# Attention with row maxima on one core: two PSUM banks for row scores and three for column scores, instead of three and two

## What is computed

```python
cov = jnp.einsum('bhsd,bhtd->bhst', qc, kc) / D
var_comp = q_var[..., :, None] * k_var[..., None, :] / D
attn = jax.nn.softmax(cov + var_comp, axis=-1)      # (32, 16, 256, 256)
out = jnp.einsum('bhst,bhtd->bhsd', attn, v)
```

## Time and profile before

| | |
|---|---|
| median of 3 runs | 1299.82 us (1298.62 to 1304.07) |
| profiled execution | 1300.59 us, of which the span from the first to the last instruction 1298.3 us |
| PE busy | 1127.0 us, 87% of the span |
| DVE busy | 989.6 us, 76% |
| ACT busy | 796.9 us, 61% |
| POOL busy | 375.9 us, 29% |
| mean granted TensorE clock | 0.972 of full speed |

### The profile page before, as it was taken

How to read it: one execution, slowest core, us unless ns; L and a number is a source line. 1 busy time by engine, 2 the same in 40 slices (tenths; PEclk the granted TensorE clock), 3 DMA queues, 4 the chain that set the end, 5 groups by cost and what they waited for, 6 DMA issues and landing times.

```text
span 1298.3 us, 33300 instructions
## 1 busy us (share of the span) xinstructions
PE 1127.0 (87%) x11462; PEld 669.0 (52%) x11462; DVE 989.6 (76%) x2827; ACT 796.9 (61%) x1440; POOL 375.9 (29%) x644
## 2 busy tenths in 40 slices
PE   1498888888888888888769999999999999999998
PEld 0234444444444444443236666666666666666676
DVE  2767887888888888876467888787888887897773
ACT  0046665666666666666647666777667677667744
POOL 5343554444445555540021011111011110011000
PEclk9999997999999999997778999999999999999999
DMA  3000000000000000000010110000000000000000
GB/s 95 5 10 15 15 17 17 17 17 17 13 17 13 17 17 17 17 11 27 5 46 1 26 26 6 20 24 24 24 19 5 24 24 24 24 11 14 18 10 17
DMA packets 50452, 24.90 MB, mean 19 GB/s; under 512 B 5984, under 2 KB 49888, under 8 KB 50400
## 3 DMA queue, kind: packets, MB, share of 16 engines
q1 hardware_dynamic: 50400, 24.21, 6.9%
HBM read 15.28 MB, written 8.39 MB: 18 GB/s over the span
## 4 chain that ended last, share of the span: by engine, by line
PE 43%; POOL 19%; ACT 17%; issue 11%; DVE 8%; ACTq 1%; POOLq 0%; DMA 0%; SPq 0%; DVEq 0%
PE bank L558 39%; ACT Kexp L1383 7%; ACT hmid L1458 4%; POOL xn L431 4%; POOL stack L461 3%; ACT prob L1361 3%; POOL sq L443 2%; DVE smax L1053 2%; PE bank L599 2%; POOL rstd L428 2%; POOL sq L445 2%; POOL stack L456 2%; ACT prob L1394 1%; POOL feat L453 1%; DVE prob L1057 1%
## 5 line engine op out<-in xcount | busy, mean ns | idle before, releaser
L975 DVE TENSOR_REDUCE rowmin<-bank 128x2 f32<-128x512 f32 x512 | 336.9, 687 | 119.0 <-PE bank L558 114.7
L1361 ACT ACTIVATE prob<-bank 128x512 f32<-128x512 f32 x512 | 301.4, 607 | 204.8 <-PE bank L558 203.8
L558 PEld LDWEIGHTS bank<-w_sb,hmid 128*128 128x128 f32 x2048 | 244.0, 192 | 24.1 <-issue 12.3
L558 PE MATMUL bank<-w_sb,hmid 128*128 128x128 f32 x2048 | 248.5, 276 | 0.2 <-issue 0.2
L1458 ACT ACTIVATE hmid<-bank,up_scale 128x512 f32<-128x512 f32 x256 | 175.9, 732 | 111.3 <-PE bank L558 111.1
L558 PE MATMUL bank<-QKT 32*128 32x256 f16 x2048 | 199.4, 285 | 31.9 <-ACT prob L1361 15.4
L1383 ACT ACTIVATE Kexp<-bank,head_bias,head_mask 128x512 f32<-128x512 f32 x256 | 187.8, 846 | 42.5 <-PE bank L558 42.5
L1266 DVE SCALAR_TENSOR_TENSOR acc<-bank,gate,acc 128x128 f32<-128x128 f32 x512 | 143.3, 342 | 72.9 <-PE bank L558 70.8
L487 POOL TENSOR_TENSOR rstd<-mv,epsilon 128x4 f32<-128x4 f32 x16 | 8.9, 553 | 503.9 <-DVE mv L1204 503.9
L558 PEld LDWEIGHTS bank<-QKT 32*128 32x128 f16 x2048 | 68.0, 94 | 155.6 <-issue 68.4
L558 PE MATMUL bank<-prob,V 128*25 128x256 f32 x2048 | 147.3, 408 | 0.0
(11 more groups left out here) (177 smaller groups left out, 1622.4 us busy)
## 6 DMA issues: line engine op xcount, KB each, us to landing
x_in<-in_L_attn_x SPq DMA_DIRECT2D x32, 128.0 KB, 2.1
z_scratch<-z_out SPq DMA_DIRECT2D x32, 128.0 KB, 1.8
xg<-in_L_attn_x SPq DMA_DIRECT2D x64, 64.0 KB, 2.0
zg<-z_scratch SPq DMA_DIRECT2D x64, 64.0 KB, 1.9
out<-acc SPq DMA_DIRECT2D x64, 64.0 KB, 1.6
QKT<-shiftT SPq DMA_DIRECT2D x128, 4.0 KB
w_sb<-in_L_ffn_w SPq DMA_DIRECT2D x1, 1024.0 KB, 6.1
wo<-in_L_attn_Wo SPq DMA_DIRECT2D x16, 4.0 KB
```

Source lines behind the costliest of these rows:

```text
L558: return pe.matmul(o, l, r, start=start, stop=stop, skip_group_check=True)
L975: dve.tensor_reduce(rowmin[h // 8][:, :, h % TILE_ROWS, h // TILE_ROWS % HALF], row_scores[i % 3][:].rearrange("p (s t) -> p s t", s=ST), ...
L1361: act.activation(prob[:, h % 8].rearrange("p t s -> p (t s)"), col_scores[h % 2][:], ACT.Exp, scale=exp_register).then_inc(s_exp, 1)
```

## The change

The first two banks go to the row scores and the next three to the column scores, and the waits follow. Row pass i now needs the reduction of two passes before, over the border of the sequences as well, since 16 is a multiple of 2. The column pass of slot h now needs the exponential of three slots before, except that slots 15 and 0 share a bank (15 % 3 = 0 % 3): at h == 0 PE waits for all exponentials of the step before, and at h == 1 and 2 for none.

```diff
-        row_scores = bank[0:3]
-        col_scores = bank[3:5]
+        row_scores = bank[0:2]
+        col_scores = bank[2:5]
...
             def row_ready(n, i):
                 if i % 8 == 0:
                     pe.wait_ge(s_half[i // 8], n + 1)
-                if i == 0:
-                    if positive(H * n):
-                        pe.wait_ge(s_max, H * n)
-                elif i >= 3:
-                    pe.wait_ge(s_max, H * n + i - 2)
+                if positive(H * n + i - 1):
+                    pe.wait_ge(s_max, H * n + i - 1)
...
             def col_ready(b, h):
                 if h % 8 == 0:
                     pe.wait_ge(s_shd[h // 8], 16 * SHIFT_DMAS * (b + 1))
-                if positive(H * b + h - 1):
-                    pe.wait_ge(s_exp, H * b + h - 1)
+                if h == 0:
+                    if positive(H * b):
+                        pe.wait_ge(s_exp, H * b)
+                elif h >= 3:
+                    pe.wait_ge(s_exp, H * b + h - 2)
```

More of the change, by code:

```diff
@@ L609, in row_ready @@
                     pe.wait_ge(s_half[i // 8], n + 1)
-                if i == 0:
-                    if positive(H * n):
-                        pe.wait_ge(s_max, H * n)
-                elif i >= 3:
-                    pe.wait_ge(s_max, H * n + i - 2)
+                if positive(H * n + i - 1):
+                    pe.wait_ge(s_max, H * n + i - 1)
             def row_pass(n, p, i, st):
                 rows, q = head_rows(row_head(i))
-                ins = mm(row_scores[i % 3][:, st * NS:(st + 1) * NS],
+                ins = mm(row_scores[i % 2][:, st * NS:(st + 1) * NS],
                          QKT[p][rows, 0, q, st * P:(st + 1) * P], QKT[p][rows, 1, q, :])
@@ L625, in col_ready @@
                     pe.wait_ge(s_shd[h // 8], 16 * SHIFT_DMAS * (b + 1))
-                if positive(H * b + h - 1):
-                    pe.wait_ge(s_exp, H * b + h - 1)
+                if h == 0:
[3 more added lines that the diff above has]
+                    pe.wait_ge(s_exp, H * b + h - 2)
             def col_pass(b, p, h, tc):
                 rows, q = head_rows(h)
-                ins = mm(col_scores[h % 2][:, tc * NS:(tc + 1) * NS],
+                ins = mm(col_scores[h % 3][:, tc * NS:(tc + 1) * NS],
                          QKT[p][rows, 1, q, tc * P:(tc + 1) * P], QKT[p][rows, 0, q, :])
@@ L975, in take_max @@
                 dve.tensor_reduce(rowmin[h // 8][:, :, h % TILE_ROWS, h // TILE_ROWS % HALF],
-                                  row_scores[i % 3][:].rearrange("p (s t) -> p s t", s=ST),
+                                  row_scores[i % 2][:].rearrange("p (s t) -> p s t", s=ST),
                                   AX.X, ALU.max, negate=True).then_inc(s_max, 1)
@@ L1360, in probabilities @@
                         act.wait_ge(s_pv, 4 * b + h // 4 - 1)
-                act.activation(prob[:, h % 8].rearrange("p t s -> p (t s)"), col_scores[h % 2][:], ACT.Exp,
+                act.activation(prob[:, h % 8].rearrange("p t s -> p (t s)"), col_scores[h % 3][:], ACT.Exp,
                                scale=exp_register).then_inc(s_exp, 1)
```

## The result

| | before | changed |
|---|---|---|
| median | 1299.22 us (1296.66 to 1304.07, 4 runs) | 1346.22 us (1343.28 to 1348.72, 4 runs) |
| profiled execution, span | 1300.59, 1298.3 us | 1345.58, 1343.3 us |
| mean granted clock | 0.972 | 0.939 |

The ratio is 1.0356, with a 95% interval from 1.0319 to 1.0394. I had forecast 1316 and a range of 1308 to 1326. The direction and the mechanism at slot 0 were right; two thirds of the loss come from something that I had given 8 in 100 and at a third of its size.

What follows compares the result with a forecast made beforehand. A loop of waits over PE, ACT and POOL was taken to set the pace. Terms 0.97 + 14.8 + 0.5 - 0.6 + 0.3 = 16.0 us on the profiled 1300.59 (0.77 above the median) led to 1316 us, range 1308 to 1326.

Steps and rivals of the forecast that it cites:

- mechanism at slot 0: Column pass, slot 0: PE waits for the exponential of head 15 instead of 14, delaying `stack`, POOL and the next step.
- Slot 0 waits for e15: Column pass, slot 0: waiting for head 15's exponential costs 0.53 us a step, +14.8 us over borders 2 to 29.
- Row side costs nothing: Row pass, slots 15, 3 and 8 need one reduction more: sum 0, at most 0.2 us a step.
- Filling: Before step 0, row passes alone: DVE may wait with two banks, 0 to 1.2 us, taken as 0.3.
- border 1: First border between steps, clock still at its lower level: slot 0 begins later, +0.97 us.
- step 29: Row pass 0 at slot 12 needs one reduction less; with no projection left, -0.6 us once.
- step 31: End of the first stage: ACT is the bound, so a third column bank gains 0.
- The third column bank pays more: Rival: the bank removes PE's waits for exponentials, 15.4 us over the run, giving 1285 or 1292; 4 in 100.
- the clock drops more often: Rival, first stage: more idle time brings more visits to 1.2 GHz, two more giving 1325 us; 8 in 100.

Runs made afterwards that it cites:

- e7: Kernel before with two row and two column banks, slot 0 waiting for the last exponential, constant products in both PE gaps (slot 0, `o_nat`): 1307.4 us.
- e2: Kernel before with the row side of the change alone (two row banks and their waits): 1303.1 us, ratio 0.999 to 1.009.
- e3: Changed kernel with the three column banks turned so that slots 15 and 0 use different banks: 1306.4 us, ratio 1.001 to 1.008.
- e4: Kernel before with two row banks, slot 0 waiting for the last exponential, two constant products on PE in front of that wait: 1348.5 us.
- e8: Kernel before with ACT's copy of `z_out` moved behind the exponential of head 14: 1312.5 us, ratio 1.005 to 1.013.
- e9: Changed kernel with ACT's copy of `z_out` moved behind the exponential of head 15: 1340.8 us, ratio 1.023 to 1.034.
- e5: Kernel before with two row and two column banks and slot 0 waiting for the last exponential, no constant products: 1354.3 us, ratio 1.038 to 1.045.
- e1: Kernel before with one edit, PE waiting at slot 0 for the exponential of head 15 too: 1350.0 us, ratio 1.035 to 1.041.
- e6: Kernel before with two row banks, slot 0 waiting for the last exponential, three constant products in front of the `o_nat` wait only: 1339.6 us.
- e12: Kernel before with two row banks, `z_out` copied behind the exponential of head 14, three constant products in front of the `o_nat` wait: 1303.7 us.

## Why the prediction was wrong, point by point

- **Slot 0 waits for e15, 0.53 us a step: right.** The step was forecast as 17.56 and was 17.5 to 17.65; PE's idle time about 0.9 and 0.91 to 1.02; POOL's 8.4 and 8.50. By e7 the term is 15.1 us for 27 steps, where the forecast's 0.53 gives 14.3. The steps of the loop take 17.53 and 17.64 in turn: slot 0 started 0.13 us behind e15 at one border and 0.25 at the other, where I had taken 0.18 for all; the unrolled steps take 17.5. One reading in this part was wrong without harm: the 0.20 us before 404.61 in the earlier trace rows is no gap of ACT, which was copying `z_out` then (404.36, 0.39 us in its timeline).
- **Row side costs nothing: right**, by e2. Its slot 8 now waits for r10 (in the changed kernel it started at 323.16, and r10 ended at about 323.05), and that was absorbed.
- **Filling, border 1, step 29, step 31: not tested one by one.** Filling came out 2.3 us shorter and the stretch between the stages 3.7 longer, against the +1.2 of these terms in my sum; their clock differs too (0.75 and 0.72), and both differences are smaller than the spread of these stretches over the runs. At border 1 the clock of the changed kernel was already up (a slot of 0.39 us, in the kernel before 0.61), so no run shows the 0.97.
- **The third column bank pays more: refuted**, by e3, which has the bank without the wait: its full-clock steps are 0.10 us shorter, and its total is 1306.
- **The step that failed is the clock's.** The forecast took over the one visit of the kernel before and made "the clock drops more often" a rival of 8 in 100 with two more visits, 9.4 us. It was the main effect: 12 more, 29.7 us (some 2.4 us each in most of the 13 long steps, not the 4.68 of the single one). The argument against it, that PE had been idle 2.55 us in each step and kept its clock, counted those steps as 26 independent trials. They were one: all had the same length, and whatever decides the fall will have come out much the same each time. I treated the clock as depending on idle time and the change as adding a little of it; e4 and e8, with less idle time per step than the kernel before and 13 and 4 visits, show that the amount was not what counted. What makes a gap a bad one stays open. The Trainium skill's rule ("TensorE: Matmul & The Clock Gate", section "A second HAM failure mode: psum-queue depth-cycling") says that brief frequent idling makes the clock swing; the trace after agrees, with 13 long steps of 27, and the trace before, with one, does not.

## What to carry to other kernels

When the number of buffers doesn't divide the number of passes, look at where the turn closes: two neighbours in one buffer undo all that the extra buffer was for. A full clock in a periodic kernel is not evidence of a margin: where TensorE idles in every period (here gaps of 0.4 and 1.3 us before the change, 1.0 and 1.3 after), the clock may come down with an edit that changes the period by a few per cent in either direction, as it did here at 1% shorter and at 3% longer, so a forecast of such a change needs a second case at the lower clock, with its price taken from the rows and for every second period. Try an edit that looks right and comes out slower once more with the gaps filled before it is thrown away.

## What the runs showed of the hardware

- The clock fell behind gaps of PE of 0.9 to 1.3 us, either of two, and not in each period. In one profiled execution each, steps of 16.8 to 17.0 us met it 4 times (e8) and twice (e3) in 27, one of 17.03 once, one of 17.04 to 17.06 never, and steps of 17.5 to 17.65 did so 12 to 17 times with `o_nat`'s gap open (e9, e5, e4, e1 and the changed kernel) and 9 times with slot 0's alone (e6). With steps of 16.8 to 17.0 and 0.2 to 0.3 us of idle time at slot 0, constant products that filled `o_nat`'s 1.32 us down to 0.46 were enough to keep it up (e12).
- Adding three or four products of PE per step to the first stage made the second one 15 to 27 us longer, with gaps of 1.5 to 2.7 us that nothing released in each turn of its loop and 78 instead of 32 packets of instructions; five did not. The runs don't show why; where the code comes to lie is my guess.
- The row of the 1.02 us at slot 0 names the right releaser, the one of slot 8 in the earlier trace rows doesn't: it names DVE's r10, for which PE didn't wait before the change; the exponential of head 6, for which it did, ended at 414.10, 0.13 us before the slot. It is the same with slot 0 in the run e6_fill_merge, whose row above names DVE: the exponential of head 15 ended at 309.55, 0.13 us before it.
